# A branch hint at the top of every turn of the ODE loops, on PE, ACT and DVE

## What is computed

```python
f = lambda z: _mlp(z, *params)          # h = tanh(z W1' + b1); h = tanh(h W2' + b2); h W3' + b3
k1 = f(y)
k2 = f(y + dt / 2 * k1)
k3 = f(y + dt / 2 * k2)
k4 = f(y + dt * k3)
return y + dt * (k1 + 2 * k2 + 2 * k3 + k4) / 6
...
_, ys = jax.lax.scan(interval, y0, None, length=S - 1)
```

## Time and profile before

| what | value |
|---|---|
| median of 3 runs | 7402.35 us |
| lowest and highest | 7397.22 and 7410.38 us |
| the profiled execution's own time | 7409.71 us |
| its span, first to last instruction | 7408.1 us |
| PE busy in the span | 6150.2 us (83%) |
| mean granted clock of PE | 0.953 |

### The profile page before, as it was taken

How to read it: one execution, slowest core, us unless ns; L and a number is a source line. 1 busy time by engine, 2 the same in 40 slices (tenths; PEclk the granted TensorE clock), 3 DMA queues, 4 the chain that set the end, 5 groups by cost and what they waited for, 6 DMA issues and landing times. The chain is left out here.

```text
span 7408.1 us, 484226 instructions
## 1 busy us (share of the span) xinstructions
PE 6150.2 (83%) x209243; PEld 3871.9 (52%) x209243; DVE 2626.0 (35%) x12603; ACT 1732.9 (23%) x8390; POOL 775.5 (10%) x1419
## 2 busy tenths in 40 slices
PE   6857999999999999997888888888888888888731
PEld 5524555555555555554875555555555555555520
DVE  5334554445544121111432222322222222222257
ACT  0122333333333333331001111111111111111111
POOL 0011111111112880000000000000000000000000
PEclk9978999999999999997999999999999999999975
DMA  1011111111111110000321111111111111111100
GB/s 45 0 49 33 33 33 33 33 34 33 33 33 36 41 42 0 0 0 14 129 75 7 7 7 7 7 7 7 7 7 7 7 7 7 7 7 7 20 13 7
DMA packets 753811, 162.32 MB, mean 22 GB/s; under 512 B 699987, under 2 KB 716791, under 8 KB 753742
## 3 DMA queue, kind: packets, MB, share of 16 engines
q1 hardware_dynamic: 702414, 86.78, 7.9%
q0 software_dynamic: 47872, 54.13, 2.7%
q10 hardware_dynamic: 3456, 20.48, 0.7%
HBM read 132.89 MB, written 28.16 MB: 22 GB/s over the span
## 5 line engine op out<-in xcount | busy, mean ns | idle before, releaser
L1667 PE MATMUL ps_rows<-whh,h_pair 128*4 128x384 f16 x34944 | 1533.5, 326 | 92.3 <-issue 1.6
L1072 PE MATMUL ode_busy<-ode_busy_x,ode_busy_w 128*32 128x384 f16 (+2 forms) x17216 | 1116.9, 326 | 22.3 <-issue 13.8
L1667 PEld LDWEIGHTS ps_rows<-whh,h_pair 128*4 128x4 f16 x34944 | 754.3, 84 | 688.3 <-DVE h_pair L1565 157.2
L1066 PEld LDWEIGHTS ode_psa<-ode_a,ode_w2t 128*32 128x32 f32 x19968 | 422.5, 109 | 707.8 <-ACT ode_a L1175 562.8
L1577 DVE COPY gate_rows<-ps_rows_last 128x128 f32<-128x128 f32 x624 | 182.2, 292 | 1670.5 <-PE ps_rows_last L1667 1670.5
L1614 ACT COPY gate_rows<-ps_rows 128x384 f32<-128x384 f32 x624 | 298.9, 479 | 1906.0 <-PE ps_rows L1667 1906.0
L1185 DVE SCALAR_TENSOR_TENSOR ode_part<-ode_b 128x1 f32<-128x1 f32 x624 | 111.3, 178 | 1607.3 <-ACT ode_b L1177 1607.3
L1177 ACT ACTIVATE ode_b<-ode_psa 128x1 f32<-128x1 f32 x2496 | 427.5, 171 | 878.7 <-PE ode_psa L1066 878.7
L1066 PE MATMUL ode_psa<-ode_a,ode_w2t 128*32 128x1 f32 x19968 | 607.7, 180 | 0.3
L1083 PE MATMUL ode_pso<-whh 125*32 125x170 f32 (+3 forms) x9600 | 565.4, 311 | 26.3 <-issue 26.2
L1175 ACT ACTIVATE ode_a<-ode_psu 128x1 f32<-128x1 f32 x1872 | 320.9, 171 | 589.5 <-PE ode_psu L1066 589.5
(11 more groups left out here) (493 smaller groups left out, 9683.4 us busy)
## 6 DMA issues: line engine op xcount, KB each, us to landing
xg_buf<-xg_scratch SPq DMA_DIRECT2D x1248, 16.0 KB, 2.0
split_raw<-in_whh_t SPq DMA_DIRECT2D x64, 256.0 KB, 2.6
ig_w<-in_wih_t SPq DMA_DIRECT2D x8, 2048.0 KB, 11.4
xg_scratch<-ig_out ACTq DMA_DIRECT2D x16, 832.0 KB, 3.5
xg_scratch<-ig_out ACTq DMA_DIRECT2D x8, 836.0 KB, 3.4
whh<-h_scratch SPq DMA_DIRECT2D x105, 62.5 KB, 2.2
h_scratch<-mlp_h SPq DMA_DIRECT2D x40, 125.0 KB, 2.3
whh<-up_scratch,whh POOLq DMA_INDIRECT x208, 5.5
```

The lines of the kernel that those rows point to most:

```text
L1066: m = nc.tensor.matmul(ps[32 * j:32 * j + 32, 0:1], w[:, 32 * j:32 * j + 32], col, start=start, stop=stop, skip_group_check=True)
L1072: nc.tensor.matmul(ps_busy[32 * j:32 * j + 32, 0:cols], busy_w[:, 32 * j:32 * j + 32], busy_x[:, 0:cols], start=True, stop=True, skip_grou ...
L1667: m = nc.tensor.matmul(out[32 * j:32 * j + 4, :], hpair[:, c, 2 - 2 * part:6 - 2 * part], whh[:, at + lo:at + hi], start=(part == 0 and c ...
```

## The change

A new helper makes a loop for one engine with the flag `hint_back_edge`. With the flag, the first instruction of every turn on that engine is a branch hint which names the loop's closing compare-and-branch and says that it will go back to the loop's beginning. The six loops of PE, ACT and DVE in the ODE layer use it. Nothing is removed, and no wait, matmul or buffer is different.

```diff
+def hinted_loop(nc, engine, start, end):
+
+    return nc.Fori(start, end, engines=bass.OrderedEngineSet([engine]), hint_back_edge=True)
...
-                with pe.Fori(0, SHADOW) as i:
+                with hinted_loop(nc, nc.tensor.engine, 0, SHADOW) as i:
                     steps_tensor(pe, i, job_slot, lambda r, s: job_gap(pe, i, r, s))
...
-                with a.Fori(0, SHADOW) as i:
+                with hinted_loop(nc, nc.scalar.engine, 0, SHADOW) as i:
...
-                with v.Fori(0, SHADOW) as i:
+                with hinted_loop(nc, nc.vector.engine, 0, SHADOW) as i:
...
-                with pe.Fori(SHADOW, STEPS // UN) as i:
+                with hinted_loop(nc, nc.tensor.engine, SHADOW, STEPS // UN) as i:
...
-                with a.Fori(SHADOW, STEPS // UN) as i:
+                with hinted_loop(nc, nc.scalar.engine, SHADOW, STEPS // UN) as i:
...
-                with v.Fori(SHADOW, STEPS // UN) as i:
+                with hinted_loop(nc, nc.vector.engine, SHADOW, STEPS // UN) as i:
```

## The result

| | before | after |
|---|---|---|
| median, same chip, 8 runs each | 7401.59 us | 7421.67 us |
| lowest and highest | 7396.72 and 7410.38 us | 7414.73 and 7437.15 us |
| ratio, 95% interval | | 1.0027 (1.0016 to 1.0038) |
| profiled execution, its span | 7409.71, 7408.1 us | 7421.73, 7420.1 us |

The change costs 20.1 us by the medians, between 12 and 28 us by the interval. The profiled execution of before was among the slowest of its runs, so the two traces lie 12.0 us apart.

A forecast was written before the change was run, and what follows sets the result against it. The chain of evaluations bounds the ODE layer, with PE's stream last at each turn's border. No saving plus 156 hints of 69 ns, 10.8 us, on the 7402.35 us median gives 7413 us; range 7396 to 7434 us.

The forecast's parts named there:

- The place: At PE's back edge in both loops, PE's instruction stream arrives last, so hint time goes one to one into the total.
- The saving: At PE's back edge, zero, since code stays loaded and no fetch is hidden; at most 132 ns.
- The rival in which the branch becomes quicker: PE's back edge saves 132 ns against the 69 ns hint: -9.8 us, 7392.5 us; chance 0.09.
- the reload rival: PE's hint loads code each turn and evicts needed blocks: 6.7 us x 154, about 1,030 us; chance 0.02.
- The size of the hint: At the top of PE's turn, one hint costs 37 + 32 = 69 ns.
- the equal split of the 95 ns: In PE's border gap, 95 ns is shared by three hand-overs (to branch, MOVE, load), 32 ns each.
- The product with 156 turns: Over both loops on PE, 156 x 0.069 = 10.8 us, shadow borders counted at the second loop's rate.
- ACT and DVE: Their loop hints add nothing: ACT has 0.26 us of cover, DVE waits 3.62 or 3.71 us.
- The clock: Rival: longer border gaps bring half-clock stretches to the shadow loop, 16.6 us more, 7430 us; chance 0.14.
- Theory B: Follow-up theory: much of the loss comes from PE's granted clock falling to half more often; no size given.
- My likeliest case: Whole kernel within 0.2% of before, chance 0.65; slower by over 0.2% had 0.29, faster 0.06.

The follow-up runs named there:

- the rotated one: Kernel before without hints, PE's first filler issued at the end of the previous turn, ahead of the branch: 7672.61 and 7672.58 us, ratios 0.9905 and 0.9924.
- the runs of equal clock: First-chip runs at mean granted clock 0.954: kernel before 7411.0 us, hints on PE alone 7423.1 us, changed kernel 7425.9 us.
- the two-turn kernel: Kernel before with two turns in the body of PE's second loop: 8105.34 us without a hint, 8132.23 us with the hint there.
- the first four experiments: On one chip: kernel before unchanged 7410.66 us; hints on PE alone 7425.12, on ACT and DVE alone 7409.57; changed kernel again 7427.56.

## Why the prediction was right, and where it was off

**The place.** Right, in the second loop one to one; in the shadow loop the place is right but part of the loss came back, as told below. The back edge of PE lies in the chain: in the second loop idle time 0.26 to 0.35 us, step 4.58 to 4.65 and 4.70 us, with 4.26 inside a turn unchanged. The kernel with the hint on PE alone shows the same loss, and the rotated one shows what the place is worth.

**The saving.** Right that there is none: 43 packets, and no fetch in the loops. The rival in which the branch becomes quicker has fallen, as the branch went from 208 to 223 ns. The price of the reload rival was read from a window of 24.0 us that is wider than the turn: from tanh to tanh the second loop's first turn took 22.8 us. That touches neither the sum nor the range. The statement of the Trainium skill ("Runtime: NRT & Kernel Launch", instruction fetch mechanics) that gives PE room for 2048 instructions agrees with both bodies: some 1,440 stay, some 2,900 do not. The same section's two blocks of 256 do not fit: by them a body of 1,440 would have waited at every border, and its branch took 208 ns with no packet in the queue.

**The size of the hint.** This is the term that was mis-sized. I had put 69 ns: the MOVE's 37 and one hand-over of 32. Measured from the start of the branch to the first weight load behind it, median over all borders of a trace, the gap went from 327 to 425 ns, 98 ns more. From hint to MOVE it is 89 ns, of which the hint's own record is 31; the next instruction starts 16 ns later behind the slower branch; and MOVE to load is 7 ns shorter. So the hint's record is as short as I thought, and the time between it and the MOVE is 58 ns, not 32. The step that failed is the equal split of the 95 ns into three hand-overs. The trace of before already had the hand-over by itself: from the end of the branch to the start of the MOVE 58 ns, and from the start of the MOVE to the load only 62, of which its record is 37.

**The product with 156 turns** came out closer than its factor, and that is luck: a price that was too low stood against a shadow loop that was counted too high. In the second loop 55 turns cost 5.9 us, 0.107 us each, about the gap's 0.098. In the shadow loop the first evaluation of a turn became 0.15 us longer (1.354 to 1.506 us between tanhs) but the second 0.09 us shorter (1.151 to 1.065): there the tanh into `b_col` had started 150 to 153 ns behind the end of the matmuls in the three traces without a hint on PE where the shadow loop is quick, and starts 67 ns behind it in the three with one. The net is 0.042 us a turn, 4.1 us in 98. I had counted the shadow border at the second loop's rate; why the other 0.09 us came back was not found. Both loops from first tanh to last took 2744.0, 2750.0 and 2742.5 us without and 2756.8, 2756.2 and 2761.6 us with hints on PE, 12.7 us more in the mean, against 10.8 forecast. About 2 of these are in the second loop's first turn, 27.2 us in one trace and 22.4 to 23.5 in the other five. The medians of the runs moved by 20.1, 13.3 and 15.8 us. The first is 7 us above what the trace accounts for and its interval begins at 12 us, so I leave that difference to the spread of runs, and claim no cause.

**ACT and DVE.** Right, on both counts: 0.31 us from matmuls to tanh, and 0.9998 for their hints alone.

**The clock.** The forecast of this rival, stretches at half clock in the shadow loop, did not come true: its clock is 1.00. In the second loop there are 7, 8 and 6 such stretches without hints on PE (35 us at half clock in the mean) and 8, 9 and 9 with them (40 us), which is worth 1 to 2 us and could be chance for one hint; with two hints there are 12 (61 us). The direction of cause was right all the same: they follow the idle time at the border, and went with it in the rotated kernel. Theory B is at most a small part of the loss, as the runs of equal clock show.

**The numbers.** 7413 us was forecast, and measured was 7421.67, inside 7396 to 7434. Of the rise of 20.1 us in the medians the forecast had 10.8, little more than half. My likeliest case was no more than 0.2% slower. Measured was 0.27%. The text had put that border at a hint of 95 ns, and it took 98; but as the shadow loop gave less than that rate, the 0.27% does not come from the 98 ns alone.

## What to carry to other kernels

Look at the instruction queue before a branch hint is tried: where no packets move inside the loop and the branch takes 0.2 us, there is no fetch to save. Even where the branch waited 3.7 us, the hint at the top of the body saved nothing here. It is one more instruction, and its price depends on its place: about 0.1 us a turn where the chain waits for what stands behind it, next to nothing in the middle of queued work. Where a loop's border shows as "issue" idle on the engine that the chain needs, move ready work ahead of the branch rather than making the branch cheaper: in the second loop the rotated turn took away nearly all of the border's 0.32 us, and the clock's falls with it. Count a new sequencer instruction by the pitch to its neighbour and not by its record.

## What was not expected

- The hinted branch was slower: medians of 216 to 223 ns against 208. That the hint does it is not shown: without any hint the branch takes 215 ns in both loops of the rotated kernel, and also in the shadow loop of the two-turn kernel whose second loop alone has the hint.
- From one sequencer instruction of PE to the next 89 ns (the hint) to 98 ns (the ALU_OP) pass, although their records are 31 and 32 ns.
- A semaphore increment at the top of the body cost no instruction and no time: 484226 instructions in both, gap 321 ns against 327, and 320 and 321 ns also stand in two traces without it.
- Two chips ran the same kernel 4.5% slower than the chip of the first four experiments did. By the traces it is the shadow loop (granted clock 0.83 against 1.00), while the second loop took 962 to 967 us without a hint at its top wherever it was traced.
- In the body that does not stay loaded, the granted clock was 0.71 in the loop, where PE stood idle for up to 4.2 us at a time. That these waits bring the low clock, so that a fetch costs twice, fits the falls at the borders but was not tested.
